# Two-layer graph attention on one core: the second layer's projection laid out by head and evicted in one operation, and the eighth query tile normalized out of PSUM

## The reference, cut to what matters

```python
h = jnp.maximum(_layernorm(x, axis=-1), 0.0)
q = (h @ W).reshape(B, N, H, D)
e_src = jnp.einsum('bnhd,d->bnh', q, a_src)
e_dst = jnp.einsum('bnhd,d->bnh', q, a_dst)
e = e_src[:, :, None, :] + e_dst[:, None, :, :]
e = jnp.where(e >= 0, e, 0.2 * e)
e = jnp.where(mask, e, NEG_INF)
attn = softmax(e, axis=2)
h_prime = jnp.einsum('bijh,bjhd->bihd', attn, q)
x = x + elu(h_prime.reshape(B, N, H * D))
```

## Time and profile before

| what | us |
|---|---|
| median of 3 runs | 4141.56 |
| lowest and highest | 4134.57, 4146.01 |
| profiled execution, its own time | 4135.93 |
| its span | 4134.1 |
| first exponent of the second layer (L1613) starts at | 2787.3 |
| TensorE, VectorE, ScalarE, GpSimd busy | 3882.4, 3513.9, 2779.1, 2440.7 |

### The profile page before, as it was taken

The page is one execution under the profiler, slowest core; times in us unless marked ns, Lnnn a source line. Parts: engine busy times, 40 slices in busy tenths (PEclk is TensorE's granted clock), DMA queues, the critical chain, the costliest instruction groups (busy, mean ns, idle before and its releaser), DMA issues. The chain is left out here.

```text
span 4134.1 us, 167624 instructions
## 1 busy us (share of the span) xinstructions
PE 3882.4 (94%) x72712; PEld 3228.9 (78%) x72712; DVE 3513.9 (85%) x5974; ACT 2779.1 (67%) x3088; POOL 2440.7 (59%) x1893
## 2 busy tenths in 40 slices
PE   7999999999999999999999999979898998999988
PEld 5877777777777787777777777758888888888887
DVE  5888888788788788888878878869999999999899
ACT  5655555555555555555555556539899998998987
POOL 4453455345354355345534534339988989889897
PEclk9999999999999999999999999989999999999999
DMA  6110110111011011011011100111213122132121
GB/s 133 30 28 22 33 33 23 33 28 33 28 28 28 23 38 28 20 36 33 23 33 28 33 22 26 43 39 45 82 41 90 52 70 87 35 91 68 49 77 39
DMA packets 170002, 178.77 MB, mean 43 GB/s; under 512 B 7184, under 2 KB 157072, under 8 KB 169104
## 3 DMA queue, kind: packets, MB, share of 16 engines
q1 hardware_dynamic: 166144, 156.08, 13.2%
q0 software_dynamic: 3088, 11.54, 1.3%
HBM read 107.02 MB, written 34.62 MB: 34 GB/s over the span
## 5 line engine op out<-in xcount | busy, mean ns | idle before, releaser
L829 ACT ACTIVATE slot<-slot,shift 128x1024 f32<-128x1024 f32 x1024 | 1077.2, 1085 | 933.0 <-PE slot L675 931.8
L514 POOL TENSOR_TENSOR ctx_sum<-ctx_sum,parts 128x256 f32<-128x256 f32 x896 | 651.0, 735 | 1327.3 <-DVE parts L989 1326.9
L968 DVE SCALAR_TENSOR_TENSOR probs<-slot,bound 128x1024 f32<-128x1024 f32 x1024 | 1243.6, 1218 | 95.8 <-ACT slot L829 89.0
L687 PEld LDWEIGHTS outs<-v_s,probs 128*64 128x64 f32 x32768 | 1007.5, 137 | 243.8 <-issue 166.1
L687 PE MATMUL outs<-v_s,probs 128*64 128x66 f32 x32768 | 1090.9, 223 | 43.0 <-DVE parts L989 30.8
L1723 DVE SCALAR_TENSOR_TENSOR p_dve<-t_ps,b_small,mask 128x1024 f32<-128x1024 f32 x832 | 1045.4, 1277 | 89.3 <-ACT t_ps L1613 78.7
L1613 ACT ACTIVATE t_ps<-s_all,d_rel 128x1024 f32<-128x1024 f32 x832 | 917.5, 1116 | 107.8 <-DVE p_dve L1723 94.2
L674 PE MATMUL slot<-q_hl,k_hl 128*128 128x512 f32 x2048 | 883.5, 431 | 28.5 <-DVE probs L968 20.4
L675 PE MATMUL slot<-q_hl,k_hl 128*128 128x512 f32 x2048 | 806.0, 394 | 0.0
L1442 POOL TENSOR_SCALAR p_pool<-r_all,b_big,b_small 128x1024 f32<-128x1024 f32 x192 | 726.2, 3782 | 43.6 <-ACT r_all L1605 31.4
L674 PEld LDWEIGHTS slot<-q_hl,k_hl 128*128 128x128 f32 x2048 | 384.7, 188 | 149.9 <-DVE probs L968 38.8
(11 more groups left out here) (150 smaller groups left out, 3939.2 us busy)
## 6 DMA issues: line engine op xcount, KB each, us to landing
q_hl<-q_hl SPq DMA_DIRECT2D x128, 256.0 KB, 3.6
s_all<-s_turned SPq DMA_DIRECT2D x64, 512.0 KB, 5.5
x_q_s<-in_x SPq DMA_DIRECT2D x32, 512.0 KB, 4.6
x<-y SPq DMA_DIRECT2D x32, 512.0 KB, 3.1
t_o_s<-x SPq DMA_DIRECT2D x16, 1024.0 KB, 5.3
out<-t_o_s SPq DMA_DIRECT2D x16, 1024.0 KB, 7.9
x_q_s<-x SPq DMA_DIRECT2D x28, 512.0 KB, 7.1
probs<-in_adj POOLq DMA_DIRECT2D x12, 512.0 KB, 7.1
```

The lines of the kernel that those rows point to most:

```text
L514: nc.gpsimd.tensor_tensor(ctx_sum[:, :, h, :], ctx_sum[:, :, h, :], parts[:, adds_before(i) % PARTS, :, :], ALU.add).then_inc(ctx_added, 1)
L687: end = nc.tensor.matmul(outs[i % OUTS][rows_of, q, 0:V_COLS], probs[:, i % PROBS, r, q * P + g * D:q * P + (g + 1) * D], v_s[:, c * JC + ...
L829: nc.scalar.activation(slot[:, :, :], slot[:, :, :], ACT.Exp, bias=shift[:, 0:1], scale=SCALE).then_inc(act_done, 1)
L968: nc.vector.scalar_tensor_tensor(probs[:, i % PROBS, :, :], spot(kind, "step", s, i)[:, :, :], P_LOW, bound[:, c % 2, :, :], ALU.max, ALU. ...
```

## The change

The 264 columns of W with its sums are put in another order: by head, 64 + e_src + e_dst, H_W = 66 to a head. A query row of a head becomes Q_H = 67 wide: the one comes first, then 64 features, e_src and e_dst; the 66 columns that the products read are the one, the features and e_src. `keep_q` is one ScalarE operation of 264 elements into `q_all`, one buffer per batch parity with all four heads (batch 0's rows stay in `near_0` and `far_0`, written by `keep_q1` in two operations). `sd` is written for batch 0 only; the other batches read e_src and e_dst out of `q_all`, strided. W is loaded by two DMAs (one for each 128 rows), 256 bytes to a piece instead of 1024.

The copy to `tail` is gone. Behind step 2 `invert_tail` takes the reciprocal of the eighth sum out of PSUM and `invert` that of the other seven; behind step 3 `keep_tail` scales the eighth tile out of PSUM into `v` and raises `tail_kept`; behind step 4 `weighted` scales the seven. DEFER becomes 4 and RING 7.

```diff
+H_W = D + 2
+WIDE = H * H_W
+Q_H = H_W + 1
+Q_W = 2 * Q_H
...
-                        sp.dma_start(w1_s[:, :, 0:F], w.rearrange("(c p) o -> p c o", p=P)).then_inc(w1_loaded, 16)
+                        for c in range(KC):
+                            sp.dma_start(w1_h[:, c, :, 0:D], w[c * P:(c + 1) * P, :].rearrange("p (h d) -> p h d", h=H))\
+                                .then_inc(w1_loaded, 16)
...
-RING = 6
+RING = 7
-DEFER = 3
+DEFER = 4
...
-        near_1 = sb("near_1", [P, NT, Q_W])
+        q_all = [sb(f"q_all{k}", [P, NT, H, Q_H]) for k in range(2)]
-        tail = sb("tail", [P, V_COLS])
...
-                q_h = (near, far)[h // 2][b % 2][:, j, h % 2 * E1:h % 2 * E1 + V_COLS]
+                if b == 0:
+                    q_h = (near_0, far_0)[h // 2][:, j, h % 2 * Q_H:h % 2 * Q_H + V_COLS]
+                else:
+                    q_h = q_all[b % 2][:, j, h, 0:V_COLS]
...
-                for side, q in enumerate((near, far)):
-                    nc.scalar.activation(q[pb % 2][:, tile, 0:2 * E1].rearrange("p (h e) -> p h e", e=E1)[:, :, 0:D],
-                                         pro[:, side * 2 * D:(side + 1) * 2 * D].rearrange("p (h d) -> p h d", d=D),
-                                         ACT.Identity, bias=zero[:, 0:1], scale=rstd[:, k % 2, t:t + 1])
-                nc.scalar.activation(sd[:, :, tile, :], pro[:, F:WIDE].rearrange("p (s h) -> p s h", s=2),
+                nc.scalar.activation(q_all[pb % 2][:, tile, :, 1:Q_H], pro[:, 0:WIDE].rearrange("p (h e) -> p h e", e=H_W),
                                      ACT.Identity, bias=zero[:, 0:1], scale=rstd[:, k % 2, t:t + 1]).then_inc(pro_free, 1)
...
+            def invert_tail(b, m):
+                f = b * UNITS + m
+                dve.wait_ge(p_used, RING + (f + 1) * ND)
+                first = m % HALVES * V_COLS
+                nc.vector.reciprocal(rc[:, MAIN:HT], sums[:, HALVES, first:first + 1]).then_inc(tail_rc_done, 1)
+
             def keep_tail(b, m):
                 f = b * UNITS + m
-                dve.wait_ge(p_used, RING + (f + 1) * ND)
-                nc.vector.tensor_copy(tail[:, :], sums[:, HALVES, m % HALVES * V_COLS:(m % HALVES + 1) * V_COLS])\
+                dve.wait_ge(tail_rc_done, f + 1)
+                first = m % HALVES * V_COLS + 1
+                nc.vector.tensor_scalar(v[:, MAIN, :], sums[:, HALVES, first:first + D], rc[:, MAIN:HT], None, ALU.mult)\
                     .then_inc(tail_kept, 1)
 
             def invert(b, m):
-                f = b * UNITS + m
-                dve.wait_ge(tail_kept, f + 1)
                 acc = sums[:, m % HALVES, 0:MAIN * V_COLS].rearrange("p (q c) -> p q c", c=V_COLS)
-                nc.vector.reciprocal(rc[:, 0:MAIN], acc[:, :, D])
-                nc.vector.reciprocal(rc[:, MAIN:HT], tail[:, D:D + 1]).then_inc(rc_done, 1)
+                nc.vector.reciprocal(rc[:, 0:MAIN], acc[:, :, 0]).then_inc(rc_done, 1)
...
-                nc.vector.tensor_tensor(v[:, 0:MAIN, :], acc[:, :, 0:D], rc[:, 0:MAIN].unsqueeze(2).to_broadcast([P, MAIN, D]),
-                                        ALU.mult)
-                nc.vector.tensor_scalar(v[:, MAIN, :], tail[:, 0:D], rc[:, MAIN:HT], None, ALU.mult).then_inc(v_done, 1)
+                nc.vector.tensor_tensor(v[:, 0:MAIN, :], acc[:, :, 1:E1], rc[:, 0:MAIN].unsqueeze(2).to_broadcast([P, MAIN, D]),
+                                        ALU.mult).then_inc(v_done, 1)
...
                             if j == 2:
+                                invert_tail(*prev)
+                                invert(*prev)
+                            if j == 3:
                                 keep_tail(*prev)
-                            if j == 3:
-                                invert(*prev)
```

More of the change, by code:

```diff
@@ L204, in layer0_block @@
         w1_s = both.w_s[:, :].rearrange("p (c o) -> p c o", c=KC)
+        w1_h = both.w_s[:, :].rearrange("p (c h e) -> p c h e", c=KC, h=H)
         wv_s = sb("wv_s", [P, KC, F])
@@ L806, in keep_q1 @@
                 own = slice(2 * pair, 2 * pair + 2)
[L807 to L810, removed]
+                nc.scalar.activation(q_near[:, own, :].rearrange("p t (h e) -> p t h e", e=Q_H)[:, :, :, 1:Q_H],
+                                     slot[:, :, 0:2 * H_W].rearrange("p t (h e) -> p t h e", e=H_W), ACT.Copy)
+                nc.scalar.activation(q_far[:, own, :].rearrange("p t (h e) -> p t h e", e=Q_H)[:, :, :, 1:Q_H],
+                                     slot[:, :, 2 * H_W:4 * H_W].rearrange("p t (h e) -> p t h e", e=H_W),
                                      ACT.Copy).then_inc(act_done, 1)
@@ L1028, in weights1 @@
                                 dve.wait_ge(w1_chain, 2 * c + 1)
-                            op = nc.vector.tensor_reduce(w1_s[:, c, F + k * H:F + (k + 1) * H], wa[:, k, :, :], AX.X, ALU.add)
+                            op = nc.vector.tensor_reduce(w1_h[:, c, :, D + k], wa[:, k, :, :], AX.X, ALU.add)
                             if k == 1:
@@ L1063, in layer1_first @@
                         nc.vector.tensor_copy(sd[:, :, 2 * pair:2 * pair + 2, :],
-                                              spot(kind, "p1", pair)[:, :, F:WIDE].rearrange("p t (k h) -> p k t h", k=2))\
+                                              spot(kind, "p1", pair)[:, :, 0:WIDE].rearrange("p t (h e) -> p t h e", e=H_W)[:, :, :, D:H_W]
+                                              .rearrange("p t h k -> p k t h"))\
                             .then_inc(slot_free, 1)
@@ L1198 @@
 T_PAIRS = IT // 2
-Q_W = 2 * E1 + 1
 MAIN = HT - 1
@@ L1253, in layer1_block @@
         h_t = sb("h1_t", [P, KC, STRIP])
-        near_1 = sb("near_1", [P, NT, Q_W])
-        near = [both.x_s[:, 0:NT * Q_W].rearrange("p (t e) -> p t e", t=NT), near_1[:, :, :]]
-        far = [both.h_s[:, k * NT * Q_W:(k + 1) * NT * Q_W].rearrange("p (t e) -> p t e", t=NT) for k in range(2)]
+        near_0 = both.x_s[:, 0:NT * Q_W].rearrange("p (t e) -> p t e", t=NT)
+        far_0 = both.h_s[:, 0:NT * Q_W].rearrange("p (t e) -> p t e", t=NT)
+        q_all = [sb(f"q_all{k}", [P, NT, H, Q_H]) for k in range(2)]
         sd = both.sd
@@ L1416, in _ @@
                                     base=0, pattern=[[-1, P]], channel_multiplier=1).then_inc(consts_ready, 1)
-            for q in (near[1], far[1]):
-                nc.gpsimd.memset(q[:, :, D:D + 1], 1.0)
-                nc.gpsimd.memset(q[:, :, E1 + D:Q_W], 1.0).then_inc(ones_ready, 1)
+            for q in q_all:
+                nc.gpsimd.memset(q[:, :, :, 0], 1.0).then_inc(ones_ready, 1)
             pool.wait_ge(ones_ready, 2)
@@ L1697, in relative @@
                 top = d_top[:, :].unsqueeze(1).to_broadcast([P, NT, H])
[L1698 removed]
+                d_col = sd[:, 1, :, :] if pb == 0 else q_all[pb % 2][:, :, :, E1 + 1]
+                nc.vector.tensor_tensor(d_rel[:, pb % 2, :, :], d_col, top, ALU.subtract).then_inc(d_rel_done, 1)
                 if pb > 0:
[L1700 removed]
+                    nc.vector.tensor_tensor(w_col[:, :, :], q_all[pb % 2][:, :, :, E1], top, ALU.add).then_inc(w_added, 1)
             def bounded(pb):
@@ L1804, in _ @@
                 batch(b, b == B - 1)
-            for closing in (keep_tail, invert, weighted, elu_low, elu_high):
+            for closing in (invert_tail, invert, keep_tail, weighted, elu_low, elu_high):
                 closing(B - 1, UNITS - 1)
```

17 lines of the change are left out of this document (7 added, 10 removed).

## The result

| | before | after |
|---|---|---|
| median of 6 runs, us | 4140.72 | 4116.85 |
| lowest and highest | 4134.57, 4146.94 | 4113.57, 4126.20 |
| span of the profiled execution | 4134.1 | 4120.1 |
| second layer, from its first exponent to the end | 1346.9 | 1327.0 |

The ratio is 0.9947, 95% interval 0.9937 to 0.9958: 22 us faster, 24 by the medians. Forecast were 30.5, range 4094 to 4130. Three later series of the kernel before, run beside the experiments, have medians of 4136.43 to 4138.11, against which 4116.85 is 20 to 21 us less. In the two profiles the second layer gave 19.9 us, while the first one, where next to nothing changed, ended at 2793.1 instead of 2787.3. So units are compared here, not spans.

What follows compares the result with a forecast made beforehand. TensorE (94% busy), VectorE (85%) and ScalarE (67%) were taken to bound different second-layer units. Savings of 11.7 + 5.3 + 3.6 + 1.4 + 0.8 + 1.8 + 5.9 = 30.5 us from 4141.56 gave 4111, range 4094 to 4130.

Steps and rivals of the forecast that it cites:

- The price of an eviction: ScalarE's copy-out of a projected token tile: one 264-element operation at 0.45 us replaces three taking 0.93, saving 0.48 per tile.
- Unit 2: Second-layer unit with projection and ScalarE busy throughout: falls from 23.36 to 21.69 us, 11.7 us over 7 batches.
- the first rival: More is taken than counted, in units 1, 3, 4, 5 and the last batch: 9 us more, 4102; chance 0.20.
- Unit 5: Second-layer unit with projection: TensorE's 0.75 us pause behind a VectorE mask goes with the eighth-tile change, 5.3 us in all.
- Unit 1: Second-layer unit with ScalarE's 2 us residual operation: the eighth-tile change saves half of some 0.4 us, 1.4 over seven.
- Unit 7: Second-layer unit shared by VectorE and ScalarE: scaling of median duration 0.38 us, saving 0.25 each, 1.8 over seven.
- Last batch: Batch without side work, VectorE setting units 3 to 7: the eighth-tile change saves 5.9 us over units 1 to 7.
- The price of the new tail: VectorE's eighth query tile from PSUM: scaling 0.22 us, 0.14 start to start; inversion of one element 0.08.
- Everything that moved: Reordered inversions, later freeing of the eighth tile's bank, longer mask ring, extra weight load, strided reads: costed at nothing.
- slower rival: TensorE reaches the eighth tile's first product before its scaling is done, 1.24 us per unit: 4163; chance 0.03.
- ScalarE's part is hidden: TensorE and the projection's single PSUM bank also hold unit 2, or eviction isn't cheaper: 11.7 us lost, 4123; chance 0.12.
- The tail isn't cheaper: The eighth tile's new scaling still waits as before, through SBUF: only 11.7 us come, 4130; chance 0.07.

Runs made afterwards that it cites:

- no_residual_op: Changed kernel without ScalarE's 2048-element residual operations in the second layer, the first layer storing its result less one: 4111.29 us, ratio 0.9933.
- evict_only: Changed kernel with the eighth tile again copied to SBUF and scaled from there, deferral 3, ring 6, keeping the single 264-element eviction: 4122.13 us, ratio 0.9966.
- tail_only: Kernel before with only the eighth tile inverted and scaled out of PSUM, deferral 4, ring 7, three evictions kept: 4135.35 us, ratio 0.9996.
- spread_io_old_tail: The spread kernel with the old tail again (copy to SBUF, scaling from there, deferral 3, ring 6): 4105.19 us, ratio 0.9916.
- after_defer3: Changed kernel with deferral 3 instead of 4 and ring 6 instead of 7: 4116.14 us, ratio 0.9947.
- spread kernel: no_residual_op with output stores and residual loads spread over the units in smaller pieces instead of 4 MB in units 0 and 1: 4096.6 us, ratio 0.9902.
- tail_one_port: evict_only with the eighth tile scaled by a two-tensor operation taking the minimum with a PSUM operand (output altered): one run, 4117.62 us.

## Why the prediction was right, and where it wasn't

The sign, the range and the two mechanisms held; of 30.5 us, 24 came by the first medians, 20 to 21 by the later ones and 19.9 in the layer's profiles. The largest shortfalls are units 1, 2 and 5. By the steps, by the medians of the table where nothing else is said:

- **The price of an eviction**: 0.45 forecast, 0.47 measured, 568 ns for "near 560".
- **Unit 2**: 1.67 forecast, 1.18 measured. I let it fall to unit 4's length since 1.9 us of ScalarE were saved; no_residual_op shows that the 2 us residual operation still held it by 0.9.
- **Units 3 and 4**: nothing forecast, 0.1 and 0.2 measured, as the first rival had it. TensorE is the cover there; the 38 us of new waits for its projection are where most of ScalarE's 54 us went.
- **Unit 5**: 0.75 forecast, 0.52 measured, by the wrong part. "The pause of 0.75 us goes with the second part" is the step that failed. I followed the wait one hop, from TensorE to a mask, found a long scaling before the mask, and stopped. The next hop was ScalarE waiting for TensorE. evict_only has the gain, tail_only hasn't.
- **Unit 0**: 0.52 forecast, 0.51 measured. **Unit 1**: 0.2 forecast, by the median nothing in the changed kernel, by the mean 0.73 lost, and 0.5 back in tail_only. Over six batches the mean makes this the largest shortfall, 5.6 us. Units 0 and 1 together took 41.3 us before, 41.5 after, 41.8 in evict_only and 41.7 in tail_only in the mean, and 40.15 without the transfers: what VectorE saved in unit 0 didn't leave the pair, because TensorE pauses during the 4 MB of transfers. The pauses stood in the windows and waits of the kernel before; I took unit 0 for VectorE's alone and unit 1 for ScalarE's. spread_io_old_tail shows both units' 0.5 once they are VectorE's. Why the mean of unit 1 is also 0.55 above that of the kernel before in evict_only, whose unit 0 didn't change, stays open; each mean is of one profile.
- **Unit 6**: 0.1 forecast, 0.35 measured, as much in evict_only: what the eviction saved in unit 5 partly shows here. **Unit 7**: 0.25 forecast, 0.10 measured. The forecast took the duration, 0.38, less the usual overlap, but VectorE's next mask starts 0.16 behind the scaling in unit 7 of batch 3, so that there was 0.11 to save:

```profile
3450.54 0.38 DVE L1745 TENSOR_SCALAR v<-tail,rc 128x64 f32<-128x64 f32 x1
3450.70 1.28 DVE L1723 SCALAR_TENSOR_TENSOR p_dve<-t_ps,b_small,mask 128x1024 f32<-128x1024 f32 x1
```

- **Last batch**: 6.4 forecast with its unit 0, 5.1 measured, 0.8 instead of 1.0 in units 4 to 6. VectorE's busy time fell by the 1.0, from 18.81 in unit 4 to 17.81, but what it waits in a unit rose from 0.36 to 0.57:

```profile
4037.19:4055.57 18.38, 16.86 (x520) 15.88 (x518) 17.81 (x21) 15.88 (x15) 17.79 (x7) 1.00 0.13 32
```

- **The price of the new tail**: the scaling out of PSUM takes 274 ns, not the copy's 217, start to start 0.19 instead of 0.14; the inversion takes 156 ns and costs the 0.08 of the forecast.
- **Everything that moved**: costed at nothing, and after_defer3 shows nothing in the time.

The slower rival never came near: in the changed kernel TensorE has no wait for the scaling, and the waits of after_defer3 cost nothing. That ScalarE's part is hidden is refuted by evict_only, where unit 2 fell by 1.2 and the layer by 13.5. "The tail isn't cheaper" was wrong by its mechanism, as the short scalings of tail_only show. The estimates beside it from the cycle table of the Trainium skill (VectorE: DVE Perf Modes, The TRN2 errata) both lie below the durations: 318 ns for the two new operations against 274 + 156 measured, though from start to start they cost 0.27 us, and 349 for the three old ones against 217 + 113 and a scaling of 598 in the mean, which held waits for GpSimd. The kernel that this rival describes is in effect evict_only, and that gave 13.5 us of the layer instead of its 11.7. What the second part is worth depends on what surrounds it: 3.3 us of the layer on the kernel before, 6.4 on evict_only, 8.1 in the spread kernel. The first rival, that more is taken, is not what 4116.85 shows; no execution of the changed kernel was below 4113.57, and the rival had 4102.

Not settled: whether the first layer pays something. It ends at 2785.8 and 2787.3 with the old loads of W and 2787.6 to 2796.7 in the ten profiles with the new ones. All ten lie above both, but two are few against a spread of 9 us, and no kernel changed this alone.

## What to carry to other kernels

Follow a wait through every engine until it comes back to where it began, before crediting its end to an edit: here the last hop was TensorE itself, and shortening VectorE's operation beside it gave nothing. Time that an engine saves is kept only up to the next point at which it waits for another, so look at the following unit too, and at pauses there that no semaphore explains; spreading one burst of transfers, the same bytes at other times and in smaller pieces, gave 14 us. Beside a pause, read the DMA queues too. Where pauses fall into some batches and not into others, medians hide what the program pays, so that the sum of the stages has to be held against the whole. The short operation with a wide spread of durations (233 to 1887 ns for 64 elements) was waiting for another engine, and another form of it was rid of that; what it cost had to be read from start to start.

## What the runs showed of the hardware that I had not expected

- A scaling of 64 elements by VectorE, one tensor from SBUF to SBUF, took 233 to 1887 ns beside GpSimd's work (evict_only), and 265 to 275 as a two-tensor operation with the second tensor in PSUM (tail_one_port).
- In the kernel before, a scaling begun beside GpSimd's operation of 3.78 us (L1442) ended 1.24 us behind that one's start in unit 0, beside the multiplication (L1445) 0.05 us behind its end in unit 5. One begun in the last 1.1 us of the 3.78 us operation was recorded as 1.10 us long in the last batch of spread_io_old_tail, and VectorE's next mask started 0.16 us behind its start.
- TensorE paused by 1 to 3 us, with no semaphore to wait for, while 4 MB were stored and loaded in two units: 6.2 us of such waits in batch 3's units 0 and 1, 2.5 without the transfers, 3.8 with them spread. 29 of the 33 longest pauses of the changed kernel's second layer end 1.1 to 1.6 us behind the end of a 16 KB packet of the queue named instruction.
